# Expert tiles of a two-layer AdaLN network: five routing rounds, an earlier end of the attention loop, output rows issued ahead of sends, and a third set of tile buffers

## The reference, cut to what matters

```python
h = _layernorm(x) * (1 + ca) + sa
x = x + ga * attention(h)     # 16 heads of 8; q, k = softplus; causal sums of k v^T and of k;
                              # out = (q . sum kv) / (q . sum k), then @ Wo.T + bo
h = _layernorm(x) * (1 + cb) + sb
t = h * rsqrt(mean(h * h) + EPS) * norm_scale
logits = t @ gate_w + gate_b            # 8 experts, the best 2 of them, softmax over the 2
y = sum over the 2: w_e * (swiglu(t @ w1_e + b1_e) @ w2_e + b2_e)    # 128 -> 512 -> 256 -> 128
x = x + gb * (h + y)
```

## Time and profile before

| | us |
|---|---|
| Median of 3 runs | 1080.95 |
| Lowest and highest | 1080.63, 1084.54 |
| The profiled execution's own time | 1088.96 |
| Its span in the trace | 1087.2 |
| TensorE busy in the span | 868.7 (80%) |
| VectorE busy | 774.8 (71%) |
| ScalarE busy | 650.8 (60%) |
| GpSimd busy | 563.9 (52%) |
| Mean granted TensorE clock | 0.899 |

### The profile page before, as it was taken

One profiled execution on the slowest core, in us unless ns is written; L12 is line 12 of the kernel. 1 busy time (PEld: TensorE's weight loads), 2 busy tenths in 40 slices (PEclk: granted clock), 3 DMA queues, 4 the chain that ended last, 5 costly groups with the idle time before them and its releaser, 6 DMA issues.

```text
span 1087.2 us, 23320 instructions
## 1 busy us (share of the span) xinstructions
PE 868.7 (80%) x7425; PEld 665.0 (61%) x7440; DVE 774.8 (71%) x2083; ACT 650.8 (60%) x1731; POOL 563.9 (52%) x583
## 2 busy tenths in 40 slices
PE   6887935999995799999999999578663588888820
PEld 6754723544452688888888888366552467777710
DVE  4897878999975867898999999655342344455538
ACT  3473258999844657687677765267441356677610
POOL 1310047478714343388888888426627545555520
PEclk9898965999998799999999999689876689999955
DMA  5230732233230300011111111324322265455348
GB/s 147 71 83 1 204 82 92 106 115 127 96 140 8 73 2 2 9 43 32 36 44 34 37 41 36 94 84 126 96 88 80 94 199 152 147 155 152 116 181 305
DMA packets 83812, 101.30 MB, mean 93 GB/s; under 512 B 15390, under 2 KB 65497, under 8 KB 81516
## 3 DMA queue, kind: packets, MB, share of 16 engines
q1 hardware_dynamic: 66396, 77.38, 23.5%
q0 software_dynamic: 8704, 18.11, 4.8%
q10 hardware_dynamic: 8592, 4.33, 1.3%
HBM read 76.11 MB, written 23.67 MB: 92 GB/s over the span
## 4 chain that ended last, share of the span: by engine, by line
PE 35%; ACT 8%; another core or an unknown queue 7%; DVE 7%; issue 7%; SPq 2%; POOL 1%; DMA 1%; ACTq 1%; DVEq 0%; POOLq 0%
PE ps L2319 10%; PE ps L2568 4%; PE ps L2335 3%; ACT qk L1800 2%; PE ps L2588 2%; ACT nrm L1805 2%; ACT xg L1816 2%; PE ps L2384 2%; PE ps L2310 2%; PE ps L2397 1%; PE ps L2281 1%; PE ps L2330 1%; PE ps L2436 1%; ACT qd L1785 1%
## 5 line engine op out<-in xcount | busy, mean ns | idle before, releaser
L1528 POOL DMA_INDIRECT parts<-xg,dest x144 | 141.3, 981 | 111.6 <-ACT xg L1816 80.0
L1487 POOL DMA_INDIRECT rows_of<-payb,posu x128 | 144.0, 1125 | 82.1 <-issue 44.2
L1478 POOL TENSOR_TENSOR kvb<-qk,v 128x1024 f32<-128x1024 f32 x64 | 126.2, 1977 | 74.7 <-DVE qk L1913 50.3
L2229 DVE TENSOR_SCALAR qk<-ps,b 128x256 f32<-128x256 f32 x144 | 62.9, 478 | 106.8 <-remote 69.9
L1115 PE MATMUL ps<-masked,ew 128*128 128x512 f32 x256 | 130.1, 624 | 4.2 <-DVE masked L1043 3.5
L2319 PE MATMUL ps<-con,kvb 128*128 128x128 f32 x1024 | 127.7, 278 | 0.0
L2319 PEld LDWEIGHTS ps<-con,kvb 128*128 128x128 f32 x1024 | 121.1, 194 | 1.0 <-issue 1.0
L2217 DVE SCALAR_TENSOR_TENSOR f_t<-qk,nrm 128x512 f32<-128x512 f32 x72 | 49.9, 693 | 66.9 <-remote 42.3
L1043 DVE TENSOR_TENSOR masked<-f_t,wide 128x512 f32<-128x512 f32 x128 | 88.7, 711 | 9.8 <-PE ps L1115 9.5
L1800 ACT ACTIVATE qk<-ps,b 128x256 f32<-128x256 f32 x144 | 60.6, 476 | 50.2 <-PE ps L2568 24.1
L1889 DVE TENSOR_TENSOR qc<-ps,qk 128x1024 f32<-128x1024 f32 x64 | 78.0, 1219 | 17.6 <-PE ps L2319 17.6
(11 more groups left out here) (375 smaller groups left out, 2106.5 us busy)
## 6 DMA issues: line engine op xcount, KB each, us to landing
wide<-hot_dram SPq DMA_DIRECT2D x16, 1024.0 KB, 4.7
xg<-rows_of SPq DMA_DIRECT2D x72, 132.0 KB
ex<-in_w_dram SPq DMA_DIRECT2D x36, 256.0 KB
lg<-in_w_dram SPq DMA_DIRECT2D x36, 256.0 KB
toep<-taps_dram SPq DMA_DIRECT2D x16, 512.0 KB, 5.8
x_tok<-in_x_dram SPq DMA_DIRECT2D x16, 256.0 KB, 3.0
out_dram<-x_tok ACTq DMA_DIRECT2D x16, 256.0 KB, 6.3
rows<-rows_dram SPq DMA_DIRECT2D x16, 192.0 KB, 3.1
```

Of the source, the lines that this page charges most:

```text
L1478: nc.gpsimd.tensor_tensor(kv[g % KB][:, :, :].rearrange("p e (h d) -> p e h d", h=H), k_in, v_in, ALU.mult).then_inc(s["kv"], 1)
L1487: nc.gpsimd.indirect_dma_start(rows_of, bass.IndirectOffsetOnAxis(ap=posu[w % 2][:, slot, t:t + 1], axis=0), pay[w % PB][:, t, :], None).t ...
L1528: nc.gpsimd.indirect_dma_start(parts, bass.IndirectOffsetOnAxis(ap=dest[:, v % YW, c:c + 1], axis=0), yw[v % YW][:, c, :], None).then_inc( ...
```

## The change

1. ROUNDS goes from 4 to 5 and PLAN from 18 to 23. All loops over attention bodies are one pass shorter, and VectorE, TensorE and ScalarE finish sequence B-1's attention in explicit steps behind them. What the last pass did for routing goes into the first round. Every index of the drains moves by one sequence, and residual and moments are now done in rounds 0 and 1. ScalarE's copy of the last projection goes to its drain at tile 1.
2. GpSimd: place_rows stands ahead of the other steps of a v and is done at every v from 4 to 24 that isn't a multiple of three (14 tiles).
3. PADS goes; pads() and second_part() both stand ahead of tile 32.
4. From tile WIDE = 30 on, glu, lin, gs and act_t have a third buffer in kvb, and the first layer a third pair of banks (6 and 7). From tile 33 on the second layer in pass v is that of tile v-3; pass 32 has none. x_t has three buffers throughout, and rows are transposed and copied two tiles ahead instead of one.
5. Added waits: for rows loaded into the first V slots, for the attention's last events before the third bank pair and kvb are reused, and for an engine's own older results (before(v)).

The diff, without the thresholds of squares and placed (B-3 to B-4 and B-4 to B-5) and without lines in which only v % 2 becomes of(v) or v % 3. A line "@@ n @@" gives the line of the kernel before; 12 columns of indentation are cut.

```diff
@@ 1301 @@
 ROUND = 5
-ROUNDS = 4
-PADS = 4
-PLAN = 18
+ROUNDS = 5
+PLAN = 23
 X_PS, Y_PS, H_PS = 0, 1, 2
+WIDE = 30
+spare = [kvb[:, j * C * P:(j + 1) * C * P].rearrange("p (f t) -> p f t", f=2) for j in range(4)]
+for ring, more in zip((glu, lin, gs, act_t), spare):
+    ring.append(more)
+x_t.append(kvb[:, 4 * C * P:4 * C * P + SP])
+
+def of(v):
+    return v % 2 if v < WIDE else v % 3
+
+def before(v):
+    return v - 2 if v < WIDE + 2 else v - 3
+
+def second_layer(v):
+    return v - 2 if v < WIDE + 2 else v - 3 if v > WIDE + 2 else -1
+
 Q = 8
@@ 1426 @@
         for v in range(BT):
-            if v == FT - PADS:
+            if v == FT:
                 pads()
-            if v == FT:
                 second_part()
+            if v < V:
+                need(sp, "tri", B * C - C + v // 2)
             if v % V == 0:
@@ 1490 @@
 
-        for n in range(B + 1):
+        for n in range(B):
             send(n - 6, 6)
@@ 1503 @@
             send(n - 5, 5)
-        send(B - 5, 6)
-        send(B - 5, 7)
+        send(B - 6, 6)
+        send(B - 6, 7)
 
@@ 1533 @@
             r, at = divmod(v, ROUND)
+            if v >= 4 and v % 3:
+                place_rows(placed_rows)
+                placed_rows += 1
             if at == 0:
-                variance_root(B - 2 + r)
+                variance_root(B - 3 + r)
             if at == 1:
-                square_root(B - 3 + r)
+                square_root(B - 4 + r)
             if at == 4:
                 for i in range(SCATTERS if r == ROUNDS - 1 else SCATTERS // 2):
-                    send(B - 4 + r, i)
+                    send(B - 5 + r, i)
             if at == 0 and r:
                 for i in range(SCATTERS // 2, SCATTERS):
-                    send(B - 5 + r, i)
-            if v >= 3 and v % 2:
-                place_rows(placed_rows)
-                placed_rows += 1
+                    send(B - 6 + r, i)
         for v in range(placed_rows, BT):
...
@@ 1735 @@
         nc.scalar.preload_act_table_set("natural_log_exp_and_others")
-        for n in range(B + 4):
+        for n in range(B + 3):
             abs_keys(n - 3)
@@ 1759 @@
 
+        projected(B - 2)
+        spread(B - 1)
         nc.scalar.preload_act_table_set("gelu_apprx_sigmoid_and_others")
-        projected(B - 1)
         act.wait_ge(s["place"], 1)
@@ 1771 @@
             if at == 0:
-                logits_kept(B - 4 + r)
-                squares(B - 3 + r)
+                logits_kept(B - 5 + r)
+                squares(B - 4 + r)
+            if v == 1:
+                projected(B - 1)
             if at == 2:
-                normed(B - 2 + r)
-                weigh_late(B - 4 + r)
-                payload(B - 3 + r)
+                normed(B - 3 + r)
+                weigh_late(B - 5 + r)
+                payload(B - 4 + r)
             if at == 3:
-                turned_pay(B - 3 + r)
+                turned_pay(B - 4 + r)
 
@@ 1782 @@
             if v < BT:
-                done(act, "h_ps", v - 2)
+                done(act, "h_ps", v - 3)
                 done(act, "x_ps", v)
-                nc.scalar.activation(x_t[v % 2][:, :], ps[:, X_PS, 0:SP], ACT.Copy, scale=ns[:, :]).then_inc(m["x_t"], 1)
+                if v < 3:
+                    need(act, "tri", B * C)
+                nc.scalar.activation(x_t[v % 3][:, :], ps[:, X_PS, 0:SP], ACT.Copy, scale=ns[:, :]).then_inc(m["x_t"], 1)
 
...
@@ 1798 @@
                     need(act, "red", B * C)
+                done(act, "gs", before(v))
...
                                                 bias=b1[:, bass.ds(e * NF + f, 1)], scale=-1.0)
                 last.then_inc(m["glu"], 1)
-                done(act, "a", v - 2)
+                done(act, "a", before(v))
                 done(act, "glu", v)
             drain(v)
@@ 1809 @@
                 ahead = pack_of(act, v + 2)
-            if v >= 2:
-                u = (v - 2) % YW
-                grouped(act, "dest", v - 2)
-                rows_out(act, v - 2 - YW)
-                done(act, "y_ps", v - 2)
+            y = second_layer(v)
+            if y >= 0:
+                grouped(act, "dest", y)
+                rows_out(act, y - YW)
+                done(act, "y_ps", y)
                 for c in range(S):
                 last.then_inc(m["yw"], 1)
...
@@ 2122 @@
 
-        for n in range(B + 1):
+        for n in range(B):
             weighted(n - 1, 0)
-            if n == B:
-                tiles_of_experts(False)
             denominators(n - 1)
@@ 2129 @@
             weighted(n - 1, 1)
-            if n == B:
-                experts_of_tiles(False)
             logits(n - 5)
@@ 2138 @@
             weighted(n - 1, 2)
-            if n == B:
-                rows_of_tiles(False)
             states(n)
@@ 2154 @@
             divided(n - 1)
+            if n == B - 1:
+                tiles_of_experts(False)
+        weighted(B - 1, 0)
+        denominators(B - 1)
+        experts_of_tiles(False)
+        weighted(B - 1, 1)
+        rows_of_tiles(False)
+        weighted(B - 1, 2)
+        weighted(B - 1, 3)
+        divided(B - 1)
         need(dve, "beside", 3)
@@ 2159 @@
             r, at = divmod(v, ROUND)
-            if v == 0:
-                residual(B - 1)
-            if v == 1:
-                moments(B - 1)
+            if at == 0 and r < 2:
+                residual(B - 2 + r)
+            if at == 1 and r < 2:
+                moments(B - 2 + r)
             if r < ROUNDS and at == 1:
-                shifted(B - 2 + r)
-                logits(B - 4 + r)
-                largest(B - 4 + r)
-                chosen(B - 4 + r)
+                shifted(B - 3 + r)
+                logits(B - 5 + r)
+                largest(B - 5 + r)
+                chosen(B - 5 + r)
             if r < ROUNDS and at == 3:
-                placed(B - 4 + r)
-                modulated(B - 2 + r)
+                placed(B - 5 + r)
+                modulated(B - 3 + r)
             if v == PLAN:
@@ 2178 @@
             if v == PLAN + 4:
-                added(B - 4)
-            for w in range(B - 3, B):
-                if v == PLAN + 5 + 2 * (w - B + 3):
+                added(B - 5)
+            for w in range(B - 4, B):
+                if v == PLAN + 5 + 2 * (w - B + 4):
                     gated(w)
-                if v == PLAN + 6 + 2 * (w - B + 3):
+                if v == PLAN + 6 + 2 * (w - B + 4):
                     added(w)
...
@@ 2224 @@
             e = expert_of(dve, packed, v)
-            bank = H_PS + 2 * (v % 2)
+            bank = H_PS + 2 * of(v)
             done(dve, "h_ps", v)
-            done(dve, "a", v - 2)
+            done(dve, "a", before(v))
             for f in range(2):
-                last = nc.vector.tensor_scalar(lin[v % 2][:, f, :], ps[:, bank + 1, f * SP:(f + 1) * SP],
+                last = nc.vector.tensor_scalar(lin[of(v)][:, f, :], ps[:, bank + 1, f * SP:(f + 1) * SP],
                                                b1[:, bass.ds(e * NF + 2 + f, 1)], 8.0, ALU.add, ALU.min)
...
@@ 2505 @@
 
-        for n in range(B + 2):
+        for n in range(B + 1):
             logits_back(n - 6)
@@ 2528 @@
             projected(n - 2)
+        sums(B - 1, 2)
+        reduced(B - 1, 0)
+        reduced(B - 1, 1)
+        spread(B - 1)
+        sums(B - 1, 3)
+        reduced(B - 1, 2)
+        reduced(B - 1, 3)
+        projected(B - 1)
         pe.wait_ge(s["place"], 1)
@@ 2536 @@
                 done(pe, "x_t", v - 1)
+                if v == 0:
+                    need(pe, "qc", B * C - 1)
                 rows_in(pe, v)
@@ 2545 @@
                 return
-            if v == 0:
-                back(B - 1)
+            if at == 0 and r < 2:
+                back(B - 2 + r)
             if at == 1:
-                logits_back(B - 4 + r)
+                logits_back(B - 5 + r)
             if at == 2:
-                ranks(B - 4 + r)
+                ranks(B - 5 + r)
             if at == 3:
-                turn_pay(B - 3 + r)
+                turn_pay(B - 4 + r)
             if at == 4:
-                logits(B - 3 + r)
+                logits(B - 4 + r)
 
         turn(0)
-        packed = before = None
-        for v in range(BT + 2):
-            turn(v + 1)
+        turn(1)
+        for v in range(BT + 3):
+            turn(v + 2)
             if v < BT:
-                bank = H_PS + 2 * (v % 2)
+                bank = H_PS + 2 * of(v)
                 done(pe, "x_t", v)
                 pe.wait_ge(s_w1[v % WC], 16 * (v // WC + 1))
-                done(pe, "lin", v - 2)
-                done(pe, "glu", v - 2)
+                done(pe, "lin", before(v))
+                done(pe, "glu", before(v))
+                if v == WIDE + 2:
+                    need(pe, "rank", B)
+                    need(pe, "lg", B)
+                    need(pe, "pay_t", B)
+                    need(pe, "lg_t", B)
                 for f in range(NF):
```

(15 more changed lines are left out.)

27 lines of the change are left out of this document (14 added, 13 removed).

## The result

The changed kernel takes 1090.51 us (median of 8 runs, 1086.72 to 1092.22) against 1081.6 us of the kernel before, 8 runs too. The ratio is 1.0068, with a 95% interval of 1.0044 to 1.0091: 0.7% or 8.9 us slower, where 10.3 us less had been forecast and the range ended at 1085.

The account below looks back on a forecast made before the run. No engine was full; TensorE's completions were taken to arrive late during GpSimd's unbroken indirect DMAs. Terms -13 + 8.8 - 10.1 + 2 + 0 + 2 = -10.3 gave 1070.6 us in the median, range 1050 to 1085.

Parts of the forecast that it names:

- runs don't hold TensorE: Rival, chance 0.17: shorter runs of indirect DMAs gain nothing, the attention end still gains; about 1081 us.
- from about the fifth on: Reading of GpSimd's unbroken indirect DMAs: TensorE's completions reach other engines late from about the fifth DMA.
- Last attention body, -13: End of attention: one sequence's routing and eight scatters leave, ending a 6.77 us wait; -13 us, bounds -5 and -16.
- Fifth round, +8.8: Tiles 20 to 24 now carry a round: 26.5 us instead of 17.7, so +8.8; bounds 0 and +14.
- Rows ahead, -10.1: GpSimd's last run: 14 tiles placed early leave 22 DMAs instead of 30; -10.1 us, bounds -34 and +5.
- Pads +2: Pad stores moved from tile 28 to 32 delay tile 32's row loads on SyncE's queue; +2 us, bounds 0 and +8.
- third set 0: Third buffers and banks from tile 30 on free what TensorE doesn't wait for; 0 us, bounds 0 and -17.5.
- tail +2: One tile without second layer at the switch, one more link of second layer and copy at the end; +2 us.
- I apply the same difference to both: Assumed both kernels' profiled executions stand 8.0 us above their medians, turning 1078.7 into 1070.6 us.
- The third set opens the even run: Rival, chance 0.15: the third set removes 17.5 us of TensorE waits in the even run; 1053 us.
- the runs grow: Rival, chance 0.13: GpSimd's fourth-round run grows to 16, the last stays at 30, fifth round paid in full; 1092 us.
- Rows ahead empty the run: Rival, chance 0.15: only the 8 last sends stand in a row, gaining 25 us instead of 10; 1056 us.

Follow-up runs that it names:

- e2: Kernel before with output rows stored by plain DMAs in fixed places, scatter of outputs by token left out, sends still indirect: 1015.8 us, ratio 0.938.
- e3: Kernel before with GpSimd pauses of about 1 us in the last run of 30 indirect DMAs: 1083.4 us, ratio 1.0016.
- e13: Kernel before with only the shorter attention and fifth round (rows behind sends, pads at tile 28, two sets, rows transposed two tiles ahead): ratio 1.0089.
- e6: Changed kernel with rows placed as before, behind the sends at odd tiles from 3 on: 1100.07 us, ratio 1.0168.
- e5: Changed kernel with its third set of buffers and banks never used: 1090.39 us, ratio 1.0085.
- e9: Changed kernel with the pads back ahead of tile 28, the wait for the sends staying at tile 32: ratio 1.0050.
- e10: Kernel before with only its pads moved to tile 32: ratio 1.0028.
- e11: Changed kernel with rows placed at every v from 4 to 24, multiples of three too: 1081.22 us, ratio 0.9996.
- e12: Changed kernel with rows at every v from 4 to 24, pads at tile 28 and short GpSimd pauses of 0.24 us: 1065.0 us, ratio 0.9844.
- e8: Kernel before with a GpSimd step of 0.24 us ahead of every placed tile and every second send: 1076.3 us, ratio 0.9953.

## Why the prediction was wrong

**The reading of the bottleneck was right.** TensorE's completions come late while GpSimd issues indirect DMAs without a break: e2 took the indirect rows away, e3 broke the run and then showed the stand again where the run was whole. The rival that runs don't hold TensorE fell. The Trainium skill's rule that spoke for it (SBUF — State Buffer, "SBUF: two separate sides": on the engine side only the port pair that VectorE and GpSimd share makes engines wait) is about ports, and no run here tests it as such; TensorE's 25.83 us of idle time came all the same.

Two details were wrong. "Two waits end within 1.1 us of a run's last DMA" holds for the run of 12 only (795.34 and 796.41). The run of 30 ends at 850.85, and ScalarE's copy comes 3.7 us later, at 854.55. The other is "from about the fifth on". In the even run, runs of four already make the odd tiles late. GpSimd's run that goes with the earlier trace rows, and VectorE's step behind it, in the timelines of the kernel before:

```profile
960.58 0.96 POOL L1528 DMA_INDIRECT parts<-xg,dest  x1 [2.12 <-ACT xg L1816]
...
964.38 0.95 POOL L1528 DMA_INDIRECT parts<-xg,dest  x1 [0.30 <-issue]
...
966.64 0.88 DVE L2229 TENSOR_SCALAR qk<-ps,b 128x256 f32<-128x256 f32 x2 [3.59 <-remote]
```

The odd tile's first layer is recorded to end at 963.76, during the third of these four DMAs. ScalarE takes its gate half at 965.10, during the fourth, and VectorE takes the other half at 966.64, 1.3 us behind the fourth.

**Last attention body, -13.** -12.9 between the two traces, and the steps as forecast. But some 3 us of it belong to the traced execution before: between the middles of eight and ten traces, 704.3 and 694.1, it is -10.

**Fifth round, +8.8: the term that was mis-sized.** It measured +16.6 alone (e13) and 32.7 - 17.7 = +15.0 in the changed kernel. I took the mean price of a round over tiles 0 to 19 (26.5 us), but a round added to the end is one of the late kind, which took 31.6 in the earlier trace rows. That row stood there, and I used it for a bound only. In the balance of the result it shows as +11.1, since tiles 25 to 29 of before, whose place the round's tiles take, were no even five either: they took 22.0 us (864.9 to 886.9), with the wait for tile 28's rows in them.

**Rows ahead, -10.1: right as a difference, set against the wrong count.** Rows ahead are worth about 10 us in the changed kernel (e6). But I compared 22 DMAs with the 30 of before. The last sends now come five tiles later, so more tiles are finished: 36 DMAs without the rows ahead and 28 with them. ScalarE had copied tile 22 by then, not "tile 20 or so", and copied tile 23 at 848.52, inside the run. The stretch went from 51.6 to 54.5 instead of falling by 10.1; without the 4.27 us for tile 32's rows it is 50.2, 1.4 less for two DMAs fewer. The rounds in front grew by 4.6 in this trace, and by 0.5 and 1.0 in e5 and e9, which have the same code there; I had kept +5 only as a bound.

**Pads +2, third set 0, tail +2.** Right within what can be resolved: +2 to +3 (e9, e10), 0 to 2 us of gain for the third set with its tail (e5), and 27.8 for 25.8. With rows behind it is more: e6 and e13 differ by 8.5 us, in pads and third set together. I didn't separate these.

**The profiled execution.** "I apply the same difference to both" was a step of its own, and wrong: 7.4 us above the median before, 1.0 after. About 3 us of it lay ahead of tile 0 and 3 to 5 in tiles 33 to 66, outside the stands. Most of the changed kernel's 5.2 us less in tiles 33 to 66 is that, not the third set.

With these, the sum is -10 (attention, between the middles), +0.5 to +4.6 (tiles 0 to 19), +2.9, +11.1, about -1 for tiles 33 to 66 (115.6 for 117, the middle of four traces) and +2.0. Together that is +5 to +9, and the medians show +8.9. It can't be had closer: tile 0 of the kernel before started within 5.8 us, and its tiles 0 to 19 took 103.8 to 107.8.

So the step that failed is the price of the moved work. The fifth round was put at the mean of the rounds, +8.8, and measured +15.0 to +16.6; and the gain of rows ahead was counted against a last run of 30, though the run itself grows when it starts five tiles later: 28 DMAs instead of 22, so no gain where -10.1 stood.

**The rivals.** "The third set opens the even run" fell: the pitch is 3.40, not near 3.0. The slower one ("the runs grow", 1092, chance 0.13) came nearest. Its run of up to 16 in the rounds was 14, its last run "near 30" was 28, its fifth round was "paid in full". Its deciding point was wrong: 14 tiles had been placed before the last sends, not fewer than 12. So it came near by its parts, not by its reason. "Rows ahead empty the run" didn't come about; with a place at every v (e11) the last run still has 14 DMAs.

What stays open: how GpSimd's runs hold TensorE. They slow SyncE's plain stores fourfold as well (e9). In the longest runs the copy that frees TensorE comes 3.7 us (before) and 4.0 us (changed kernel, 876.67 against 872.68) behind the end of the last DMA's issue, so the end of the issuing alone doesn't end the stand. Since the ends of matmuls are modelled, the traces don't tell whether the matmuls themselves are late or only the news of them. And no run here tells whether it is in the writing of descriptors, in the DMA rings, or in the path of the semaphores.

## What to carry to other kernels

Price an added round, iteration or stage at what its neighbours at that place cost, not at the mean, and recount the queue that a later start leaves behind. An engine that issues indirect DMAs in an unbroken run can hold another that seems unrelated to it: look for waits that end with the run or shortly behind it, and give GpSimd its DMAs early, while it would idle (e11, e12), rather than all at once later. Before a sum is made against one traced execution that stands off its median, find out where it stands off.

## What was not expected of the hardware

- Plain stores on GpSimd's queue in place of 144 indirect ones took 67 us off, and left TensorE at 2.95 us a tile with no idle time (e2).
- During an unbroken run of indirect DMAs, eight plain stores issued by SyncE took 31.22 us instead of 8.00 (e9 against the changed kernel).
- A GpSimd step of 1.04 us ahead of each pair of indirect DMAs let TensorE run at 2.97 us a tile (e3). A step of 0.24 us shortened the stand from 51.6 to 38.7 us for five tiles and left the even run at 3.53 (e8).
